# A third block's experts by routed rows: scatter to DRAM, 23 tiles of 128 rows, gather back

## The chip, the core and the metric

One core of one Trainium2 chip runs the whole program. The metric is the device time of one execution in microseconds, the median of several runs. PE is TensorE (matrix products and transpositions), PEld its weight loads, DVE is VectorE, ACT ScalarE, POOL GpSimd, SP SyncE, which here only issues DMAs.

## The reference

The input is one image of 32 x 32 tokens with 128 channels, so N = 1024 tokens, T = 8 tiles of P = 128. Three blocks of attention and mixing follow each other, then the fourth: a plain attention over 1024 tokens with its own experts. The change concerns the experts of the third block, `_L2_ffn_ref`:

```python
logits = xt @ Wr + br                                  # E = 8 experts
probs = softmax(logits); top_p, top_idx = top_k(probs, 2)
weights = top_p / top_p.sum(axis=-1, keepdims=True)
xn = layer_norm(xt)                                    # no gain
xe = xn[None] * ln_g[:, None, :] + ln_b[:, None, :]    # gain and bias per expert
h = gelu(einsum('end,edh->enh', xe, W1) + b1)          # 128 -> 512
y = einsum('enh,ehd->end', h, W2) + b2                 # 512 -> 128
out = sum over the token's two experts of weights * y[expert, token]
```

All experts are written as computed for all tokens, and only two of the eight results of a token are used. Everything is float32.

## The kernel before, in words

There is one instruction list per engine, written out by hand; the engines meet at semaphores (`wait_ge` on `at(name, k)`). Within an engine the order in the list is the order of execution. Operations of DVE or POOL that depend on each other go through `link`, which waits for each one's end.

The experts of the third block are computed densely. `tokens_to_channels` turns the tokens of the normalised block input (`bK`, for the router) and of the second normalisation (`cK`, for the experts), `router` makes the logits in one PSUM bank, and `router_logits`, `rank_experts` and the lines after them on DVE make `cw`, a weight for each token and expert that is zero for all but two experts.

For each expert the input is `nT` times the expert's gain plus its bias. Both this input (1024 columns) and the first matrix (128 x 512) are split into a high and a low part, so that a product is three passes of a fast number format with 512 columns (`PASSES`): ACT makes the high part of the input, POOL the whole input (`m2_xe`, line 649) and the high part of the matrix (line 484), DVE the low parts (`x_low`, `w_low`). `experts` on PE runs the first product of expert e and then the second product of expert e - 1 (`fc2`), in plain float32, 4 calls of 128 columns for each token tile. ACT evaluates the gelu (line 847) from PSUM into `hid(e)`. `accumulate` on DVE adds `cw` times the result to the residual `aK` (line 1905) for each expert and tile, and after the last expert makes the statistics of the next normalisation (`nc`). In the trace a call of PE in float32 is two records; `mm` is line 933, `turn4` line 943.

SP loads all second matrices (2 MB, line 410) and all first ones (2 MB, line 412) during the second block, and, expert by expert as a buffer comes free, those of the fourth block's experts (lines 417 and 419).

POOL's queue around the change: it splits the heads of the third block's attention, makes the high parts, the roots of the normalisations (`token_roots`, line 463), then small tables for the fourth block, and the roots of `nc`.

Two operations of the second block read a register from SBUF and use it as an address, as the change does: `split_stacks` on POOL (`value_load` of `topi`, then line 556) and `gather_keys` on DVE (line 1717).

After the experts PE turns the normalised tokens, makes queries, keys and values for the fourth attention, and goes on as before; the change leaves that part as it is. `warm` are products without use, which keep PE's clock up.

Of the kernel before, what the change touches and what calls it, by code (L numbers as in the profile page):

```python
# [5 lines left out]
P = 128  # L6
IMG = 32
T = IMG * IMG // P
N = T * P
# [34 lines left out]
U = 64  # L44
# [6 lines left out]
BIG = 3.0e38  # L51

# [18 lines left out]
for _name, _cols in (("n0_q_b", 4), ("n0_k_b", 4), ("n1_q_b", 4), ("n1_k_b", 4), ("L0_conv_proj_b", 1),  # L71
# [22 lines left out]
                  ("nn_tps", 2), ("nd_tps", 2)],  # L94
# [4 lines left out]
                   ("nb_T", 2), ("m2_xT", 2), ("nd_T", 2)],  # L99
# [29 lines left out]
for _kind, _count in (("lg_ps", 2), ("lg", 1), ("ex", 1)):  # L129
    KINDS["expert_" + _kind] = [(f"m2_{_kind}", _count), (f"m3_{_kind}", _count)]  # L130
# [23 lines left out]
def build(nc, A, out):  # L154
    with ExitStack() as ctx:
# [150 lines left out]
        lmask = sb("lmask", [P, T], U8)  # L306
        nanm = sb("nanm", [P, T, P], U8)
# [6 lines left out]
        xpart2 = kr[:, :, :].rearrange("p (b a) n -> p b a n", b=2)  # L314
        wpart2 = qr[:, :, :, :].rearrange("p b (a c) n -> p b a (c n)", a=2)
# [68 lines left out]
        def hid(e):  # L384
            return arena[:, 4096 * (e % 2):4096 * (e % 2) + 4096].rearrange("p (c n) -> p c n", c=FC)
# [12 lines left out]
        def _(sp):  # L398
# [9 lines left out]
            sp.dma_start(fb2[:, :], A["fb2"]).then_inc(S("fb2_in"), 16)  # L408
            sp.wait_ge(*at("conv_ps", 2))
            sp.dma_start(fw2[:, :, :, :], A["m2_w2"]).then_inc(S("fw_in"), 16)  # L410
            sp.wait_ge(*at("n1_qm", T))
            sp.dma_start(fw1[:, :, :], A["m2_w1"]).then_inc(S("fw_in"), 16)

            for e in range(E):
                sp.wait_ge(*at("m2_w_high", e + 1))
                sp.wait_ge(*at("m2_w_low", e + 1))
                sp.dma_start(fw1[:, e, :], A["m3_w1"][:, e]).then_inc(S("fv_in"), 16)
                sp.wait_ge(*at("m2_fc2", 2 * (e + 1)))
                sp.dma_start(fw2[:, e, :, :], A["m3_w2"][:, e]).then_inc(S("fv_in"), 16)
# [7 lines left out]
        def _(pool):  # L427
# [202 lines left out]
            def w_high(e):  # L630

                if e == 0:
                    pool.wait_ge(*at("fw_in", 32))
                if e >= 2:
                    pool.wait_ge(*at("m2_fc1", 8 * (e - 1)))
                copy(wpart2[:, e % 2, 0, :], fw1[:, e, :]).then_inc(S("m2_w_high"), 1)

            w_high(0)
            w_high(1)
# [3 lines left out]
            for e in range(E):  # L643
                dst = (bT, cT)[e % 2]
                if e == 0:
                    pool.wait_ge(*at("m2_xT", 2))
                if e >= 2:
                    pool.wait_ge(*at("m2_x_low", e - 1))
                pool.tensor_scalar(dst[:, :], nT[:, :], col("L2_ffn_ln_g", e), col("L2_ffn_ln_b", e),
                                   ALU.mult, ALU.add).then_inc(S("m2_xe"), 1)  # L650
                if 1 <= e < E - 1:
                    w_high(e + 1)

            def count(dst, pattern, mult):
                return pool.iota(dst, pattern, base=0, channel_multiplier=mult, allow_small_or_imprecise_dtypes=True)
# [9 lines left out]
            pool.wait_ge(*at("m2_fc1", 8 * E))  # L665
            pool.memset(k_high[U:U + 1, :].bitcast(F32), 1.0).then_inc(S("n3_ones"), 1)
            pool.wait_ge(*at("n3_ones", 1))
            token_roots("nc")
# [23 lines left out]
        def _(act):  # L692
# [130 lines left out]
            def router_exp(pre):  # L823
                act.wait_ge(*at(f"{pre}_lg", 1))
                act.activation(ex[:, :, :], lg[:, :, :], ACT.Exp).then_inc(S(f"{pre}_ex"), 1)

            def expert_layer(pre, func):

                def x_high(e):

# [1281 lines left out]
```

## Time and profile before

| | us |
|---|---|
| median of 3 runs | 537.44 |
| lowest, highest | 537.29, 545.58 |
| the profiled execution | 541.85 |
| its span, first to last instruction | 539.7 |
| PE busy in the span | 482.6 (89%) |
| mean granted clock of TensorE | 0.94 of 2.4 GHz |

The profile is of one execution on this core. Times in the rows are from the start of the span, in microseconds unless marked. "Busy" leaves out register, semaphore and DMA-issuing instructions. What stands in square brackets behind an instruction is the idle time of its engine before it and what ended it.

### The profile page before, as it was taken

The page shows a single profiled execution, that of the slowest core. Times are in us where ns is not written, and L with a number is a line of the kernel's source. Part 1 is how long each engine was busy: PE and PEld are TensorE (multiplying, and loading weights), DVE is VectorE, ACT ScalarE, POOL GpSimd, SP SyncE. Part 2 cuts the span into 40 slices and gives each one's busy share as a digit, 9 for nine tenths or more (in the row PEclk, how much of TensorE's full clock was granted, in tenths as well). Part 3 has the DMA queues.
Part 4 walks back from the last instruction along what each step waited for, and adds up shares of the span by engine and source line. Part 5 has one row for each costly group of instructions (what it writes and reads, how often), then busy time and mean ns, then how long its engine had stood idle before and what let it go on. Part 6 is the DMA issues. An engine that isn't in the chain of part 4 may idle for free.

```text
span 539.7 us, 9856 instructions
## 1 busy us (share of the span) xinstructions
PE 482.6 (89%) x3723; PEld 360.1 (67%) x3723; DVE 313.4 (58%) x830; ACT 243.4 (45%) x473; POOL 132.9 (25%) x187
## 2 busy tenths in 40 slices
PE   4988999795999999975886899999999999979994
PEld 3276676433677677763575789999998444567983
DVE  3858787478856668828366742233216531367367
ACT  0838877173355555640263495444440223310630
POOL 7622236004413323213331321112003300021000
PEclk9999999799799999997799699999999958979998
DMA  8000000000000000034000001111112000000001
GB/s 292 4 2 2 1 2 1 1 2 1 1 1 2 1 1 2 2 130 182 2 1 2 19 1 41 40 39 40 40 40 58 1 0 0 2 0 0 2 1 39
DMA packets 4680, 13.49 MB, mean 25 GB/s; under 512 B 466, under 2 KB 1562, under 8 KB 4250
## 3 DMA queue, kind: packets, MB, share of 16 engines
q1 hardware_dynamic: 4634, 12.86, 7.0%
q8 instruction: 30, 0.49, 0.4%
q14 instruction: 16, 0.13, 0.1%
HBM read 12.34 MB, written 0.52 MB: 24 GB/s over the span
## 4 chain that ended last, share of the span: by engine, by line
PE 75%; DVE 14%; ACT 4%; issue 3%; POOL 2%; DMA 1%; DVEq 1%; POOLq 0%; ACTq 0%
PE ps L933 68%; PE ps L1076 3%; DVE tabs L1568 2%; PE ps L943 2%; DVE st L1552 1%; PE ps L1056 1%; POOL rstd L463 1%; DVE arena L1690 1%; DMA xT<-in_xT_dram 1%; DVE oK L1666 1%; ACT arena L812 1%; DVE nmx L1830 1%; DVE arena L1827 1%; DVEq L1716 1%; PE ps L1047 1%
## 5 line engine op out<-in xcount | busy, mean ns | idle before, releaser
L933 PE MATMUL ps<-kr,qr 128*128 128x512 f32 (+3 forms) x328 | 92.8, 399 | 6.1 <-DVE kr L1717 2.4
L933 PEld LDWEIGHTS ps<-kr,qr 128*128 128x128 f32 x328 | 61.1, 193 | 22.8 <-issue 6.5
L847 ACT ACTIVATE arena<-ps,first 128x512 f32<-128x512 f32 x64 | 42.6, 689 | 38.5 <-PE ps L933 38.5
L933 PEld LDWEIGHTS ps<-fw,arena 128*128 128x128 f32 x512 | 58.3, 192 | 0.6
L933 PE MATMUL ps<-fw,arena 128*128 128x128 f32 x512 | 58.3, 275 | 0.0
L1786 DVE TENSOR_REDUCE nmx<-ps 128x1 f32<-128x512 f32 x64 | 43.8, 686 | 22.2 <-PE ps L933 21.7
L799 ACT ACTIVATE pT<-ps 128x512 f32<-128x512 f32 x64 | 38.3, 598 | 39.9 <-PE ps L933 39.3
L1905 DVE SCALAR_TENSOR_TENSOR aK<-ps,cw,aK 128x128 f32<-128x128 f32 x64 | 18.0, 344 | 63.4 <-PE ps L933 63.4
L463 POOL TENSOR_TENSOR rstd<-ve,nhalf 128x4 f32<-128x4 f32 x14 | 14.2, 1016 | 102.2 <-DVE ve L1561 102.1
L933 PE MATMUL ps<-kr 128*128 128x512 f32 x76 | 37.4, 582 | 1.0 <-ACT kr L910 1.0
L1690 DVE CUSTOM_DVE_ANT_0 arena<-ps,tabs 128x320 f32<-128x320 f32 (+1 forms) x64 | 28.8, 459 | 14.7 <-PE ps L933 14.7
L933 PE MATMUL ps<-pT,tabs 128*32 128x128 f32 (+2 forms) x576 | 35.6, 295 | 0.7 <-ACT pT L799 0.7
L762 ACT ACTIVATE arena<-arena,nmx 128x320 f32<-128x320 f32 (+1 forms) x64 | 32.2, 534 | 1.9 <-DVE nmx L1690 1.9
L1076 PE MATMUL ps<-ident,arena 128*64 128x128 f32 (+2 forms) x176 | 30.3, 277 | 1.1 <-ACT arena L762 0.5
L933 PE MATMUL ps<-first 128*128 128x256 f32 x98 | 30.2, 464 | 1.1 <-ACT arena L750 0.7
L715 ACT ACTIVATE pT<-ps,lowbias,islow 128x512 fp32r<-128x512 f32 x32 | 24.6, 778 | 12.8 <-PE ps L933 10.9
L556 POOL TENSOR_TENSOR tabs<-vaug,ones 128x151 f32<-128x151 f32 x32 | 14.3, 447 | 64.5 <-PE ps L933 36.7
L933 PEld LDWEIGHTS ps<-kr 128*128 128x128 f32 x76 | 16.3, 221 | 19.3 <-issue 16.3
L933 PEld LDWEIGHTS ps<-first 128*128 128x128 f32 x98 | 22.2, 237 | 4.8 <-ACT arena L750 0.9
L537 POOL TENSOR_TENSOR qr<-fw,mask 128x1024 fp32r<-128x1024 f32 x8 | 15.2, 1895 | 40.6 <-PE ps L933 35.8
L933 PEld LDWEIGHTS ps<-pT,tabs 128*32 128x32 f32 (+2 forms) x576 | 18.3, 111 | 6.6 <-issue 2.0
L933 PE MATMUL ps<-kv_high,convw_high 128*128 128x512 f32 x50 | 22.1, 442 | 0.0
(311 smaller groups left out, 937.2 us busy)
## 6 DMA issues: line engine op xcount, KB each, us to landing
fw<-in_m_w_dram SPq DMA_DIRECT2D x2, 2048.0 KB, 10.3
fw<-in_m_w_dram SPq DMA_DIRECT2D x16, 256.0 KB, 3.0
convw<-in_convw_dram SPq DMA_DIRECT2D x1, 1600.0 KB, 10.5
rows<-in_rows_dram SPq DMA_DIRECT2D x1, 584.0 KB, 6.1
xT<-in_xT_dram SPq DMA_DIRECT2D x1, 512.0 KB, 3.6
out_dram<-aK SPq DMA_DIRECT2D x2, 256.0 KB, 2.3
w<-in_w_dram SPq DMA_DIRECT2D x1, 448.0 KB, 6.9
late<-in_late_dram SPq DMA_DIRECT2D x1, 360.0 KB, 10.9
```

Of the source, the lines that this page charges most:

```text
L463: pool.tensor_tensor(dst, src, nhalf[:, 0:n], ALU.pow).then_inc(S(f"{name}_root"), 1)
L537: pool.tensor_tensor(dst.rearrange("p (g a) n -> p g a n", a=2), qst[:, :, P * t:P * t + P].unsqueeze(2).broadcast_to([P, 4, 2, P]), mask[ ...
L556: pool.tensor_tensor(vfil[:, t % 2, j:j + 1, :], vaug[:, bass.ds(r, 1), :], ones[:, 0:1].unsqueeze(2).broadcast_to([P, 1, VW]), ALU.mult). ...
L715: act.activation(pT[:, u % 4, :].bitcast(F32R), ps[:, u % 4, :], ACT.Identity, bias=lowbias[:, layer, a, k:k + 1], scale=islow[:, low:low ...
L762: act.activation(v, v, ACT.Exp, bias=nmx[:, t, h:h + 1], scale=-1.0).then_inc(S("n0_p"), 1)
L799: act.activation(pT[:, u % 8, :], ps[:, 4 + u % 2, :], ACT.Exp).then_inc(S("n1_p"), 1)
L847: act.activation(hid(e)[:, c // 2, HALF * (c % 2):HALF * (c % 2) + HALF], ps[:, c % 4, :], func, bias=col("L2_ffn_b1", FC * e + c // 2)).t ...
L933: return pe.matmul(dst, lhsT, rhs, start=start, stop=stop, skip_group_check=True)
L1076: ins = pe.transpose(ps[0:n, 4 + m % 2, P * j:P * j + P], arena_s(m // NH8)[:, m % NH8, P * j:P * j + n], ident[:, :])
L1690: dve.tensor_tensor_reduce(arena_s(t)[:, h, 0:w], ps[:, s % 4, 0:w], tab[:, h, :, :].rearrange("p l j -> p (l j)"), -1.0, FMAX, ALU.add, A ...
L1786: dve.tensor_reduce(nmx[:, s // NH8, s % NH8:s % NH8 + 1], ps[:, s % N1_S, :], AX.X, ALU.max, negate=True).then_inc(S("n1_nmx"), 1)
L1905: dve.scalar_tensor_tensor(acc[:, t, :], ps[:, 4 + 2 * (e % 2) + t // 4, P * (t % 4):P * (t % 4) + P], cw[:, t, e:e + 1], acc[:, t, :], AL ...
```

## The change

The experts work on rows instead of on all tokens. A row is a token with one of its two experts, 2048 rows in all. Each expert's rows are padded to whole tiles of 128, at most (2 x 1024 + 8 x 127) // 128 = 23 tiles; 23 are always run.

1. Two tensors in DRAM are added: `x_dram`, 9 x 1024 rows of 128 (1024 for each expert), and `y_dram`, 23 x 128 rows. SP fills `x_dram` with zeros early in the program (4.7 MB).
2. DVE works out the routing in two halves of 4 tiles: for each token and expert its place among the expert's rows (PE sums over tokens with triangular and full matrices of ones, `m2_positions`), from it `row_of` for the scatter and, with the number of tiles of each expert, `back_of` for the gather, `tile_expert` and `tile_row` for each tile, and its gain, bias and first bias (`tables`, `rows_back`).
3. POOL sends the normalised rows `cK` to `x_dram` with 16 indirect DMAs of 128 rows (`send_rows`), 8 after each half.
4. SP loads the first matrix of the first 4 tiles (256 KB each, expert by register, `weights_in`) into a ring of 4 buffers, waits for all rows, loads 23 tiles of rows (64 KB, first row by register, 5 in flight), and then, tile by tile, the first matrix of tile i + 4 and the store of the result i.
5. PE turns the tile, and runs four calls of 128 columns for the first product and four for the second, all in plain float32, one step apart: turn s, first product s - 1, second product s - 2. It reads the expert of a tile into a register and uses it to address the second matrix. DVE applies gain and bias on the way out of PSUM, ACT the gelu, DVE copies the result.
6. When all 23 results are in DRAM, POOL gathers them with 16 indirect DMAs, and DVE adds them with their weights to `aK`, tile by tile, with the statistics of `nc`.
7. The dense products, the high and low parts and `accumulate` are gone. The fourth block's first matrices are loaded whole in place of the third's, its second ones after the last second product.

```diff
+            sp.wait_ge(*at("w3_sums", 1))
+            sp.dma_start(x_dram.rearrange("(a p) c -> p a c", p=P), fills[:, 0:1, :].broadcast_to([P, XROWS // P, P])
+                         ).then_inc(S("rows_zero"), 16)
             sp.wait_ge(*at("conv_ps", 2))
             sp.dma_start(fw2[:, :, :, :], A["m2_w2"]).then_inc(S("fw_in"), 16)
             sp.wait_ge(*at("n1_qm", T))
-            sp.dma_start(fw1[:, :, :], A["m2_w1"]).then_inc(S("fw_in"), 16)
-            for e in range(E):
...
+            sp.dma_start(fw1[:, :, :], A["m3_w1"]).then_inc(S("fv_in"), 16)
+            def weights_in(i):
+                if i >= W1_BUFS:
+                    sp.wait_ge(*at("m2_fc1", i - W1_BUFS + 1))
+                e = sp.value_load(tile_expert[0:1, i:i + 1], min_val=0, max_val=E - 1)
+                sp.dma_start(w1_of(i), A["m2_w1"][:, bass.ds(e, 1), :].rearrange("p a h -> p (a h)")
+                             ).then_inc(S(f"w1_in_{i % W1_BUFS}"), 16)
+            sp.wait_ge(*at("tile_row", 1))
+            for i in range(W1_BUFS):
+                weights_in(i)
+            sp.wait_ge(*at("rows_out", 16 * TOPK * T))
+            for i in range(NT):
+                if i >= IN_FLIGHT:
+                    sp.wait_ge(*at(f"rows_in_{i % IN_FLIGHT}", 16 * (i // IN_FLIGHT)))
+                sp.dma_start(x_rows[:, i, :], x_dram[bass.ds(tile_row_of(i), P), :]).then_inc(S(f"rows_in_{i % IN_FLIGHT}"), 16)
+            for i in range(NT):
+                if i + W1_BUFS < NT:
+                    weights_in(i + W1_BUFS)
+                sp.wait_ge(*at("m2_y", i + 1))
+                sp.dma_start(y_dram[P * i:P * i + P, :], y_rows[:, i, :]).then_inc(S("y_stored"), 16)
+            sp.wait_ge(*at("m2_fc2", NT))
+            sp.dma_start(fw2[:, :, :, :], A["m3_w2"]).then_inc(S("fv_in"), 16)
@@ POOL
+            def send_rows(i):
+                pool.wait_ge(*at("row_of", i + 1))
+                pool.wait_ge(*at("nn_norm", 4 * i + 4))
+                for t in range(4 * i, 4 * i + 4):
+                    for r in range(TOPK):
+                        pool.indirect_dma_start(out=x_dram[:, :], out_offset=bass.IndirectOffsetOnAxis(
+                            ap=row_of[:, r, t:t + 1], axis=0), in_=cK[:, t, :], in_offset=None,
+                            bounds_check=XROWS - 1, oob_is_err=False).then_inc(S("rows_out"), 16)
...
+            pool.wait_ge(*at("y_stored", 16 * NT))
+            for t in range(T):
+                for r in range(TOPK):
+                    pool.indirect_dma_start(out=y_back[:, r, t, :], out_offset=None, in_=y_dram[:, :],
+                                            in_offset=bass.IndirectOffsetOnAxis(ap=back_of[:, r, t:t + 1], axis=0),
+                                            bounds_check=NT * P - 1, oob_is_err=False).then_inc(S(f"y_back_{t // 2}"), 16)
@@ PE
+            for s in range(NT + 2):
+                if s < NT:
+                    pe.wait_ge(*at(f"rows_in_{s % IN_FLIGHT}", 16 * (s // IN_FLIGHT + 1)))
+                    if s >= 2:
+                        pe.wait_ge(*at("m2_xt", s - 1))
+                    pe.transpose(ps[:, s % 2, 0:P], x_rows[:, s, :], ident[:, :]).then_inc(S("m2_xt_ps"), 1)
+                    e_of[s] = pe.value_load(tile_expert[0:1, s:s + 1], min_val=0, max_val=E - 1)
+                i = s - 1
+                if 0 <= i < NT:
+                    pe.wait_ge(*at("m2_xt", i + 1))
+                    pe.wait_ge(*at(f"w1_in_{i % W1_BUFS}", 16 * (i // W1_BUFS + 1)))
...
+                    for c in range(FC):
+                        ins = mm(ps[:, 2 + i % 2, P * c:P * c + P], w1_of(i)[:, P * c:P * c + P],
+                                 x_turned[:, i % 2, :])
+                    ins.then_inc(S("m2_fc1"), 1)
+                i = s - 2
+                if 0 <= i < NT:
...
+                    pe.wait_ge(*at("m2_h", FC * (i + 1)))
+                    for c in range(FC):
+                        ins = mm(ps[:, 4 + i % 2, 0:P], hid[:, i % 2, c, :], fw2[:, bass.ds(e_of[i], 1), c, :],
+                                 start=c == 0, stop=c == FC - 1)
+                    ins.then_inc(S("m2_fc2"), 1)
@@ DVE, in this order
+            router_logits("m2", 0, 4, 0, 4, 1)
+            rank_half(0)
+            half_stats("nn", bK, 1, "nb")
+            normalise_half("nn", bK, cK, 0)
+            rows_of_half(0)
+            router_logits("m2", 0, 2, 4, T, 2)
+            rank_half(1)
+            normalise_half("nn", bK, cK, 1)
+            rows_of_half(1)
+            tables()
+            rows_back()
...
+            for s in range(NT + 2):
+                if s < NT:
+                    dve.wait_ge(*at("m2_xt_ps", s + 1))
...
+                    dve.tensor_scalar(x_turned[:, s % 2, :], ps[:, s % 2, 0:P], tile_gain[:, s:s + 1], tile_bias[:, s:s + 1],
+                                      ALU.mult, ALU.add).then_inc(S("m2_xt"), 1)
+                i = s - 2
+                if 0 <= i < NT:
+                    dve.wait_ge(*at("m2_fc2", i + 1))
+                    dve.tensor_copy(y_rows[:, i, :], ps[:, 4 + i % 2, 0:P]).then_inc(S("m2_y"), 1)
```

## Rows read from the trace of the kernel before

**Rows 1.** The page: PE's busy time, and the chain that ended last by engine
```profile
PE 482.6 (89%) x3723; PEld 360.1 (67%) x3723; DVE 313.4 (58%) x830; ACT 243.4 (45%) x473; POOL 132.9 (25%) x187
PE 75%; DVE 14%; ACT 4%; issue 3%; POOL 2%; DMA 1%; DVEq 1%; POOLq 0%; ACTq 0%
```

**Rows 2.** Stages: stretch and length, busy PE, PEld, DVE, ACT, POOL, clock, DMA, GB/s
```profile
310.80:412.40 101.60, 101.60 (x718) 93.71 (x719) 32.26 (x90) 49.40 (x71) 14.76 (x19) 1.00 0.13 37
```

**Rows 3.** Groups of PE from 310 to 413, by form: count, busy us, mean ns, idle
```profile
L933 PE MATMUL ps<-fw,arena 128*128 128x128 f32 x512 | 58.3, 275 | 0.0
L933 PE MATMUL ps<-kr,qr 128*128 128x512 f32 x180 | 43.3, 395 | 0.9 <-ACT arena L847 0.9
```

**Rows 4.** Timeline at both ends of the stage: start us, us, engine line operation
```profile
293.01 0.29 DVE L1843 TENSOR_TENSOR aK<-ps,aK 128x128 f32<-128x128 f32 x1 [0.31 <-PE ps L933]
297.45 0.87 DVE L1552 BATCH_NORM_STATS2 st<-tabs 128x6 f32<-128x128 f32 x4
298.10 1.72 PE L933 MATMUL ps<-late,oT 128*128 128x8 f32 x8
298.71 1.11 DVE L1568 TENSOR_SCALAR tabs<-tabs,mv,rstd 128x128 f32<-128x128 f32 x4
...
412.33 1.13 DVE L1905 SCALAR_TENSOR_TENSOR aK<-ps,cw,aK 128x128 f32<-128x128 f32 x4 [1.06 <-PE ps L933]
```

**Rows 5.** Timeline of DVE: two router operations and two of the ranking
```profile
307.95 0.22 DVE L1863 TENSOR_REDUCE lm<-lg 128x8 f32<-128x64 f32 x1
308.20 0.22 DVE L1864 TENSOR_TENSOR lg<-lg,lm 128x64 f32<-128x64 f32 x1
308.46 0.69 DVE L1873 TENSOR_TENSOR tabs<-lg 128x512 f32<-128x512 f32 x1
309.19 0.69 DVE L1874 TENSOR_TENSOR tabs<-tabs,tril 128x512 f32<-128x512 f32 x1
```

**Rows 6.** SP's DMA issues in the timeline, and by size with us to landing
```profile
329.54 0.33 SPq L419 DMA_DIRECT2D fw<-in_m_w_dram  x1
329.96 0.38 SPq L417 DMA_DIRECT2D fw<-in_m_w_dram  x1
...
fw<-in_m_w_dram SPq DMA_DIRECT2D x2, 2048.0 KB, 10.3
fw<-in_m_w_dram SPq DMA_DIRECT2D x16, 256.0 KB, 3.0
out_dram<-aK SPq DMA_DIRECT2D x2, 256.0 KB, 2.3
```

**Rows 7.** Registers read from SBUF, on POOL and DVE; POOL's operation on 128x1024
```profile
209.06 0.44 POOL L556 TENSOR_TENSOR tabs<-vaug,ones 128x151 f32<-128x151 f32 x1 [0.73 <-POOL tabs L556]
210.23 0.53 POOL L556 TENSOR_TENSOR tabs<-vaug,ones 128x151 f32<-128x151 f32 x1 [0.72 <-POOL tabs L556]
L1717 DVEq FUSED_REGOPS  x2: 69/69/69, 125.7 to 126.5; - x2
L537 POOL TENSOR_TENSOR qr<-fw,mask 128x1024 fp32r<-128x1024 f32 x8 | 15.2, 1895 | 40.6 <-PE ps L933 35.8
```

**Rows 8.** Timeline: four transpositions on PE, four 128-column operations on ACT
```profile
273.67 0.60 PE L943 MATMUL ps<-ident,arena 128*128 128x128 f32 x4
275.21 1.28 ACT L812 ACTIVATE arena<-arena,nmx 128x128 f32<-128x128 f32 x4 [1.86 <-DVE nmx L1830]
```

**Rows 9.** Stages of 5 us: PE's busy time is the second number, its clock third last
```profile
275.00:280.00 5.00, 4.26 (x39) 4.10 (x38) 3.05 (x9) 3.84 (x12) 2.27 (x3) 1.00 0.01 2
295.00:300.00 5.00, 3.12 (x17) 2.79 (x18) 4.70 (x28) 1.20 (x2) 2.67 (x3) 0.78 0.00 0
300.00:305.00 5.00, 4.83 (x19) 4.23 (x20) 2.98 (x7) 3.25 (x4) 1.90 (x2) 0.50 0.18 52
```

**Rows 10.** Timeline: a DVE cast beside a POOL operation that reads SBUF
```profile
126.90 2.99 POOL L545 TENSOR_TENSOR tabs_parts<-tabs,kv_high 128x1296 fp32r<-128x1296 f32 x1
127.02 3.15 DVE L1717 CAST kr<-arena 128x512 fp32r x1
```

More of the change, by code:

```diff
@@ L129 @@
 for _kind, _count in (("lg_ps", 2), ("lg", 1), ("ex", 1)):
-    KINDS["expert_" + _kind] = [(f"m2_{_kind}", _count), (f"m3_{_kind}", _count)]
+    KINDS["expert_" + _kind] = [(f"m2_{_kind}", 2 if _kind == "lg" else _count), (f"m3_{_kind}", _count)]
+for _kind, _first, _second in (("fc1", NT, 2 * E), ("fc2", NT, E), ("h", FC * NT, FC * E), ("y", NT, E)):
+    KINDS["expert_" + _kind] = [("m2_" + _kind, _first), ("m3_" + _kind, _second)]
+KINDS["constants"] = [("rpb_zero", 1), ("gavg_ready", 1), ("shift_ready", 1), ("ident_ready", 2), ("rmask_ready", 1),
+                      ("islow_ready", 1)]
+KINDS["gathered"] = [("m3_gathered", T), ("slotrow_ps", 1)]
+KINDS["hot_made"] = [("m3_hot_ready", T), ("m3_xg_dve", 1)]
+KINDS["slots_made"] = [("m3_before", 2), ("m3_slot", 1)]
+KINDS["route_ps"] = [("m2_pos", 2), ("m2_count", 1), ("m2_cwt_ps", 2), ("m2_b2_ps", 2), ("m3_pos", 1)]
+KINDS["m2_sums"] = [("m2_cw", 1), ("m2_b2", 2), ("m2_acc", T)]
+KINDS["n3_prepared"] = [("places_ready", 4), ("w3_twice", 1), ("n3_ones", 1), ("n3_k_high", 2)]
+KINDS["expert_chosen"] = [("m2_chosen", 2), ("m3_hot", 1)]
+KINDS["m2_tables"] = [("row_of", 2), ("tile_expert", 1), ("tile_row", 1), ("tile_b1", 1), ("back_of", 1)]
 for _group in (("ln1", "nb", "nc", "nd"), ("ln2", "nn")):
@@ L306, in build @@
         lmask = sb("lmask", [P, T], U8)
+        row_of = sb("row_of", [P, TOPK, T], U32)
+        back_of = sb("back_of", [P, TOPK, T], U32)
+        tile_expert = sb("tile_expert", [P, NT], U32)
+        tile_row = sb("tile_row", [P, NT], U32)
         nanm = sb("nanm", [P, T, P], U8)
@@ L1330, in _ @@
             warm(2, 5)
             tokens_to_channels("nb_tps", (0, 1), bK, "nb_norm")
-            router("m2", 0, 4, oT, "nb_T", range(0, 4))
-            tokens_to_channels("nn_tps", (2, 3), cK, "nn_norm")
-            router("m2", 0, 4, oT, "nb_T", range(4, T))
-            warm(2, 5)
-            pe.wait_ge(*at("m2_xT", 2))
-            def m2_w(e, second):
-                pe.wait_ge(*at("fw_in", 32))
-            def m2_parts(e):
-                for name in ("m2_x_high", "m2_x_low", "m2_w_high", "m2_w_low"):
-                    pe.wait_ge(*at(name, e + 1))
@@ L1345, in _ @@
-            experts("m2", m2_parts, m2_w)
+            for i in range(2):
+                router("m2", 0, 4 - 2 * i, oT, "nb_T", range(4 * i, 4 * i + 4))
+            for i in range(2):
+                m2_positions(i)
+            for i in range(2):
+                ins = mm(ps[:, 6, 0:E], ones[:, :], half_sum[:, i, :], start=i == 0, stop=i == 1)
+            ins.then_inc(S("m2_count"), 1)
+            pe.wait_ge(*at("m2_cw", 1))
+            for i in range(2):
+                for j in range(4):
+                    ins = pe.transpose(ps[0:E, 4 + i, P * j:P * j + P], cw[:, 4 * i + j, :], ident[:, :])
+                ins.then_inc(S("m2_cwt_ps"), 1)
@@ new lines, in rows_back @@
+            def rows_back():
+                link(dve.scalar_tensor_tensor(row_step, start_of, float(P), first_row, ALU.mult, ALU.subtract))
+                link(dve.tensor_tensor(row_terms, rank_is, row_step.unsqueeze(1).unsqueeze(1).broadcast_to([P, TOPK, T, E]),
+                                       ALU.mult))
+                link(dve.tensor_reduce(weight, row_terms, AX.X, ALU.add))
+                dve.tensor_tensor(back_of[:, :, :], row_no, weight, ALU.add).then_inc(S("back_of"), 1)
+                dve.wait_ge(*at("back_of", 1))
```

357 lines of the change are left out of this document (188 added, 169 removed).

## The prediction

> **What bounds the kernel now.** I read the page's busy line and its chain first, then the stages, the groups of PE, and the timeline at both ends of the stage that is replaced. PE is busy 89% of the span and holds 75% of the chain that ended last [rows 1]: what PE does not do in this kernel is saved, as long as nothing else takes the time. The third block's experts are the stretch 310.8 to 412.4: PE is busy in all 101.6 us of it, at a granted clock of 1.00 (2.4 GHz), with DVE at a third and ACT at a half [rows 2]. Its work is 256 calls of the second product (512 records, 58.3 us, so 0.228 us a call) and 192 products of 512 columns, mostly in 43.3 us [rows 3]. The stage begins earlier on the other engines: the last residual of the attention is added at 293.01, the router's first half is out of PE at 298.10 + 1.72 = 299.8 at a low clock, and the last accumulation starts at 412.33 [rows 4]. I work the new course out on this clock and compare its end with 412.33.
>
> **What goes.** All of the dense products, the splits into high and low parts, and eight accumulations per tile. The time from the router's logits to the last accumulation, 412.33 - 299.8 = 112.5 us, is what the new course has to beat.
>
> **Row numbers on DVE.** A small operation on 64 elements takes 0.22 and starts 0.25 apart; one on 512 takes 0.69 and starts 0.73 apart [rows 5]. For 256 elements I estimate 0.45, between them. Each half of the router: three small (0.75), five of 256 (2.25), three small (0.75), together 3.75; then four operations for the rows, 1.0. The first half also has the statistics of the second normalisation, 1.27, and each half four normalised tiles, 1.11 [rows 4]. So the first row numbers are ready at 299.8 + 3.75 + 1.27 + 1.11 + 1.0 = 307.0, the second at 307.0 + 3.75 + 1.11 + 1.0 = 312.9. The tables follow: tile_expert and tile_row after 11 operations of 0.27, at 315.9; biases, rows_back and weights about 6.6 more, 322.5; for the transposed weights and their product with the second bias, PE, ACT and DVE in turn, I allow 5 us. DVE enters the tile loop at about 327.4. That is under the scatter, and costs nothing unless the scatter ends before 325.
>
> **Scatter.** POOL issues 16 indirect DMAs, one after another on its queue. The trace has none. The nearest rows are SP's plain DMA issues, 0.33 and 0.38, with starts 0.42 apart [rows 6], and POOL's gather of values, which reads a register out of SBUF and runs one operation: starts 1.17 apart, of which 0.73 is idle before it [rows 7]. An indirect DMA must read 128 numbers and write descriptors for them, so 0.42 is the low end; the high end, 2.0, is by POOL's slowest frequent operation, the one on 128x1024 at 1.90 [rows 7]. I take 1.2, near the row that also reads an index. Eight from 307.0 end at 316.6, past the second half's 312.9, so all 16 end at 307.0 + 19.2 = 326.2; with a landing of 2.3, the store's row [rows 6], the rows are in DRAM at 328.5.
>
> The Trainium skill, "DMA: Bandwidth & Descriptors", section "Latency and other measured facts", gives a first byte of about 1 us on this path, with the Q7's emission as its reason. No row here shows it. If 1.0 were the spacing, the sum below would be 6.4 us lower.
>
> **Loads of the rows.** The part that I think least visible: SP issues all 23 row loads before it issues weight 4. Each reads a register from SBUF and then issues a DMA that uses it. I put the register at 0.7: it is the 0.73 that POOL stands before the operation that follows one, and DVE's queue, which does the same, shows its register operations 0.8 apart, 125.7 and 126.5 [rows 7]. With an issue of 0.38 [rows 6] and a short wait that makes 1.15 a load, bounds 0.75 (the read partly hidden) and 1.4. 23 x 1.15 = 26.5, so 355.0; weight 4 is issued at 356.1 and lands 3.0 later, as 256 KB did [rows 6], at 359.1. Tiles 0 to 3 run below this and then PE stands for some 15 us. Five loads in flight are enough: five spacings are 5.75, a landing 2.3.
>
> **The tile loop.** Per tile PE has one transposition and eight calls of 128 columns: 8 x 0.228 + 0.11 = 1.94, the 0.11 from four transpositions that take 0.60 with 0.27 of it for the first [rows 8]. ACT has four gelus of 128 columns, 1.28 for four such operations [rows 8]; DVE two evacuations of 0.29 [rows 4]; SP one register, two issues and waits, 1.6; the 256 KB of a weight at the rate of the 2 MB load (10.3 us [rows 6]) 1.3. All lie below PE. PE must also read a register and form addresses: 0.65 or more, hidden as far as the sequencer runs ahead of eight queued products. No row shows PE do this. I take 0.46 of it as seen, so 2.4 a tile, bounds 1.94 and 3.0. From fc1(4) to fc2(22) are 19.5 tiles: 46.8. PE comes out of a stand, and the 5 us after one like it were granted 0.50 [rows 9], which loses some 2 us. End of fc2(22): 359.1 + 46.8 + 2 = 407.9. Evacuation, store issue and landing, 0.3 + 0.4 + 2.3: all y are in DRAM at 410.9.
>
> **Gather.** 16 indirect DMAs again, and all of them wait for the last store: 19.2 + 2.3 = 21.5, so 432.4. The accumulation of the last two tiles and their statistics, about 2.4, answer to the 2.5 that now follows 412.33 [rows 4]. So the stage ends 432.4 - 412.3 = 20.1 later. PE has stood meanwhile: the next attention's first 5 us at 0.50 cost 2.5 more [rows 9]. Sum: +22.6.
>
> The Trainium skill, "SBUF — State Buffer", section "SBUF: two separate sides", has a passage on DVE blocking DMAs from the GpSimd queue: a DVE operation that holds the shared ports keeps the descriptors from being written. The trace shows the lock from the other side, a cast taking 3.15 beside a POOL operation of 2.99 [rows 10]. By that rule the DVE operations beside the scatter and the gather, 16 of about 0.34 in the gather, would add at most 5 us; I leave it out of the sum.
>
> **Nothing for the rest.** The zeroing of the scatter's buffer (4.7 MB) is issued when the first loads are out and PE has 200 us of other work before rows are sent; at the rate above it takes 24 us of the DMA engines, idle there. The last block's 2 MB are loaded whole, 10.3 us, long before 500. Five iotas on POOL, 1 us, lie below DVE's attention work.
>
> **From the profile to the metric.** The profiled execution took 541.85: a span of 539.7 and 2.15 around it. The median is 537.44, 4.4 less. 541.85 + 22.6 = 564.4, less 4.4: 560.0 us. A measurement of this kernel tells about 2% from no change: 526.7 and 548.2.
>
> **Rivals.**
> - *Cheap indirect DMAs (not slower).* Place: POOL's queue, from the first row number to the last gather. If one costs what SP's issue does, 0.42, the scatter ends at 312.9 + 3.4 = 316.3, row loads end at 345.1, y is stored at 401.0, the last gather landed at 410.2: 2 us less than now, plus 2.5 of clock, 538 us. Each 0.1 us is 3.2 us of the total; below 0.83 the result is within 2%. With SP's loads at 0.75 (-9) and PE at 1.94 (-9) as well it is 519. For it: no POOL DMA is in the trace, so nothing excludes it. Against: 128 numbers per DMA, and the 0.73 for one [rows 7].
> - *Dear indirect DMAs*, 2.0: 32 x 0.8 = +25.6, 585 us.
> - *The tile loop loses the clock.* A stretch with PE busy 3.12 of 5 us was followed by one at 0.50, 4.26 of 5 kept 1.00 [rows 9]. At 2.4 a tile PE is busy 81%; at 3.0 it is 65%, and half clock makes the work 3.9. At a mean of 3.3 the loop is 17.6 longer: 578 us.
> - *Row loads overlap*: if SP's registers run ahead, 0.75 a load, 9.2 less: 551 us.
> - The loop's counts are constants, so routing cannot make it shorter, and that it does not do what it says I do not reckon with.
>
> **Chances.** Forecast 0.44, cheap 0.20 (0.09 of it faster by over 2%), dear 0.14, clock 0.11, overlapping loads 0.11 (half of it within 2%). The forecast's own low tail gives 0.04 to no change. Faster 0.09, within 2% 0.20, slower 0.71. The range reaches down past the cheap rival to 532 and up past the dear one to 588. The forecast's own is 549 to 574.
>
> **What would show it.** Right: POOL's indirect DMAs 1.2 apart, 16 before and 16 after the loop; SP's row loads 1.15 apart with PE idle some 15 us after tile 3; PE's tiles 2.4 apart at clock 1.00 with DVE, ACT and the DMA engines waiting; the last accumulation some 20 us later than 412.33 [rows 4]. Wrong: indirect DMAs under 0.8 apart; PE without a gap between tiles 3 and 4; a loop that waits for weights, so that the transfers and not PE set its pitch; tiles over 3 apart.

## The result, and the profile after

The changed kernel takes 555.46 us (median of 4 executions, 553.21 to 557.58) beside 538.33 for the kernel before: a ratio of 1.033, interval 1.029 to 1.037. The forecast was 560.0, range 532 to 588, slower. Run once more, later, it took 555.12 (553.91 to 566.9), ratio 1.031 [1.026, 1.036]. Some executions of most versions here are over 1.5% longer than the version's shortest, at a lower granted clock of TensorE; the ratios leave these out and the medians do not, so where they are many, as in a version below, the two say different things.

The page of the kernel after, PE's busy line and the chain that ended last by engine, answers to [rows 1]:

```profile
PE 438.6 (79%) x3420; PEld 323.3 (58%) x3420; DVE 314.4 (57%) x858; ACT 217.1 (39%) x491; POOL 151.4 (27%) x208
PE 64%; DVE 14%; issue 7%; POOL 4%; SPq 4%; ACT 3%; DMA 2%; DVEq 1%; POOLq 0%
```

PE does 44 us less work (482.6 before) and the kernel is 16 us longer: 60 us went into stretches in which PE stands. The chain says who holds it there: "issue", time in which an engine waits for nothing that the profile shows, rose from 3% to 7%, POOL from 2% to 4%, and SPq, SP's queue, is new with 4%, some 22 us.

I measure the stage from the last residual add of the attention before it to the last variance (`ve`) behind it: 293.01 to 414.68 before, 121.7 us; 299.08 to 436.20 after, 137.1 us. The stages of the kernel after inside it (columns as in [rows 2]):

```profile
299.10:314.30 15.20, 8.98 (x36) 7.49 (x35) 11.62 (x55) 1.45 (x3) 3.06 (x4) 0.50 0.00 0
314.30:339.90 25.60, 8.73 (x38) 7.42 (x39) 14.51 (x45) 1.17 (x2) 20.13 (x22) 0.50 0.28 85
339.90:351.80 11.90, 9.64 (x62) 8.47 (x62) 2.55 (x8) 5.60 (x17) 0.00 (x0) 0.81 0.21 58
351.80:367.60 15.80, 0.05 (x1) 0.08 (x1) 0.51 (x2) 0.15 (x1) 0.00 (x0) 0.59 0.27 74
367.60:408.50 40.90, 40.37 (x330) 39.17 (x331) 10.98 (x36) 21.73 (x76) 0.00 (x0) 0.95 0.53 149
408.50:436.20 27.70, 3.03 (x15) 2.32 (x13) 9.55 (x34) 0.00 (x0) 17.23 (x17) 0.64 0.35 116
```

Read the second number, PE's busy time, against the length. Routing, scatter (POOL busy 20.1), tiles 0 to 3, a stretch of 15.8 in which the computing engines do nearly nothing (0.7 busy in all), 19 tiles at PE's own pace (40.4 of 40.9), gather (POOL 17.2). Of 137 us PE works 71; before it worked 117 of 122. It stands in three stretches above all: 16.9 us beside the scatter, 15.8 behind tile 3, 24.7 in the gather. POOL's timeline has the scatter (first fence) and the gather (second):

```profile
314.26 1.47 POOL L736 DMA_INDIRECT expert_rows_dram<-tabs,row_of  x1 [1.79 <-issue]
...
323.72 0.97 POOL L736 DMA_INDIRECT expert_rows_dram<-tabs,row_of  x1 [0.30 <-issue]
325.00 1.95 POOL L736 DMA_INDIRECT expert_rows_dram<-tabs,row_of  x1 [0.30 <-issue]
327.26 1.04 POOL L736 DMA_INDIRECT expert_rows_dram<-tabs,row_of  x1 [0.30 <-issue]
...
334.98 0.97 POOL L736 DMA_INDIRECT expert_rows_dram<-tabs,row_of  x1 [0.30 <-issue]
```

```profile
411.33 1.11 POOL L758 DMA_INDIRECT arena<-expert_out_dram,back_of  x1 [72.18 <-DMA expert_out_dram<-arena]
412.74 1.01 POOL L758 DMA_INDIRECT arena<-expert_out_dram,back_of  x1 [0.31 <-issue]
...
431.09 0.99 POOL L758 DMA_INDIRECT arena<-expert_out_dram,back_of  x1 [0.30 <-issue]
```

Most scatters start 1.28 us apart (0.97 busy, 0.30 between), gathers 1.30; the first scatter takes 1.47 and the ninth 1.95. SP's timeline and then PE's show the row loads and the stand that they make; where the timeline merges instructions, the second number spans all of them:

```profile
338.00 25.78 SPq L502 DMA_DIRECT2D arena<-expert_rows_dram  x23
364.56 0.33 SPq L492 DMA_DIRECT2D xT<-in_m_w_dram  x1
```

```profile
351.50 0.27 PE L1394 MATMUL ps<-ident,arena 128*128 128x128 f32 x1
367.55 2.05 PE L1007 MATMUL ps<-arena,xT 128*128 128x128 f32 x8 [15.77 <-DMA xT<-in_m_w_dram]
...
378.30 1.06 PE L1007 MATMUL ps<-fw,arena 128*128 x8
379.19 0.27 PE L1394 MATMUL ps<-ident,arena 128*128 128x128 f32 x1
380.24 1.06 PE L1007 MATMUL ps<-fw,arena 128*128 x8
381.13 0.27 PE L1394 MATMUL ps<-ident,arena 128*128 128x128 f32 x1
```

23 row loads, 1.157 us apart; the weight of tile 4 behind the last; PE idle 15.77 us for it. From the second one on, a transposition every 1.89 to 2.10 us.

Outside the stage the two profiles differ too: the stage begins 6.1 us later (299.08 against 293.01), and from the last variance to the end it is 119.4 us, not 125.0. 15.4 + 6.1 - 5.6 = 15.9, the whole difference of the spans (555.6 - 539.7). The runs below had to tell which of these three belongs to the change.

### The profile page after: what moved, and what is told of

Same layout as the page of the kernel before. It is cut to its first block, busy times and chain, and to the rows that moved or that the text cites. A ratio compares the mean times of both kernels' runs of the same rounds, so it can differ in the third digit from the quotient of the medians.

```text
span 555.6 us, 9834 instructions
## 1 busy us (share of the span) xinstructions
PE 438.6 (79%) x3420; PEld 323.3 (58%) x3420; DVE 314.4 (57%) x858; ACT 217.1 (39%) x491; POOL 151.4 (27%) x208
## 3 DMA queue, kind: packets, MB, share of 16 engines
q1 hardware_dynamic: 21642, 24.53, 13.9%
q0 software_dynamic: 1024, 2.10, 1.3%
## 4 chain that ended last, share of the span: by engine, by line
PE 64%; DVE 14%; issue 7%; POOL 4%; SPq 4%; ACT 3%; DMA 2%; DVEq 1%; POOLq 0%
PE ps L1007 57%; PE ps L1150 3%; POOL arena L758 2%; SPq L485 2%; PE ps L1017 2%; POOL expert_rows_dram L736 2%; SPq L502 2%; DVE tabs L1637 1%; DVE st L1621 1%; PE ps L1130 1%; DVE arena L1759 1%; ACT arena L905 1%; DMA xT<-in_xT_dram 1%; DVE nmx L1899 1%; DVE arena L1896 1%
## 5 line engine op out<-in xcount | busy, mean ns | idle before, releaser
L892 ACT ACTIVATE pT<-ps 128x512 f32<-128x512 f32 x64 | 38.3, 598 | 40.4 <-PE ps L1007 39.8
L1007 PE MATMUL ps<-kr,qr 128*128 128x320 f32 (+3 forms) x136 | 46.4, 404 | 4.4 <-DVE kr L1786 2.4
L931 ACT ACTIVATE arena<-ps,convw 128x128 f32<-128x128 f32 x92 | 26.2, 370 | 35.9 <-PE ps L1007 35.9
L758 POOL DMA_INDIRECT arena<-expert_out_dram,back_of x16 | 16.2, 1012 | 76.7 <-DMA expert_out_dram<-arena 72.2
L1017 PE MATMUL ps<-ident,tabs 128*128 128x128 f32 x40 | 8.6, 354 | 35.1 <-DVE tabs L1637 35.1
L2043 DVE COPY arena<-ps 128x128 f32<-128x128 f32 x23 | 6.7, 292 | 51.4 <-PE ps L1007 51.4
L1007 PEld LDWEIGHTS ps<-kr,qr 128*128 128x128 f32 x136 | 25.4, 197 | 13.2 <-issue 5.7
L1007 PE MATMUL ps<-kr 128*128 128x512 f32 x76 | 31.3, 498 | 1.0 <-ACT kr L984 1.0
L1007 PE MATMUL ps<-arena,xT 128*128 128x128 f32 x96 | 15.5, 313 | 16.1 <-DMA xT<-in_m_w_dram 15.8
L1017 PEld LDWEIGHTS ps<-ident,tabs 128*128 128x128 f32 x40 | 6.1, 182 | 38.0 <-issue 26.6
L627 POOL TENSOR_TENSOR qr<-fw,mask 128x1024 fp32r<-128x1024 f32 x8 | 15.1, 1893 | 45.4 <-PE ps L1007 39.9
L1007 PE MATMUL ps<-fw,arena 128*128 x184 | 25.4, 282 | 1.8 <-ACT arena L931 1.3
## 6 DMA issues: line engine op xcount, KB each, us to landing
expert_rows_dram<-fills SPq DMA_DIRECT2D x1, 4608.0 KB, 18.3
convw<-in_convw_dram SPq DMA_DIRECT2D x1, 1600.0 KB, 11.2
```

Source lines behind the costliest of these rows:

```text
L627: pool.tensor_tensor(dst.rearrange("p (g a) n -> p g a n", a=2), qst[:, :, P * t:P * t + P].unsqueeze(2).broadcast_to([P, 4, 2, P]), mask[ ...
L758: pool.indirect_dma_start(out=y_back[:, r, t, :], out_offset=None, in_=y_dram[:, :], in_offset=bass.IndirectOffsetOnAxis(ap=back_of[:, r, ...
L892: act.activation(pT[:, u % 8, :], ps[:, 4 + u % 2, :], ACT.Exp).then_inc(S("n1_p"), 1)
L931: act.activation(hid[:, i % 2, c, :], ps[:, 2 + i % 2, P * c:P * c + P], ACT.Gelu, bias=tile_b1[:, i, c:c + 1]).then_inc(S("m2_h"), 1)
L1007: return pe.matmul(dst, lhsT, rhs, start=start, stop=stop, skip_group_check=True)
L1017: ins = pe.transpose(ps[0:rows, bank, cols * j:cols * j + cols], src, ident[0:cols, 0:cols])
```

## The experiments

The first four versions ran beside executions of the kernel before with a median of 539.42.

**The zero fill moved.** SP's fill of `x_dram` is issued some 240 us in, not 22.

```diff
-            sp.dma_start(x_dram.rearrange(...), fills...).then_inc(S("rows_zero"), 16)
...
             sp.dma_start(fw1[:, :, :], A["m3_w1"]).then_inc(S("fv_in"), 16)
+            sp.dma_start(x_dram.rearrange(...), fills...).then_inc(S("rows_zero"), 16)
```

> The changed kernel with one edit: the 4.6 MB that zero the scatter's buffer are issued behind the two 2 MB loads, at about 243 us, instead of at 22 us. My theory: this transfer, in flight from 22 to 40 us, is why the first attention starts at 45.3 instead of 40.6 (a gap of 0.87 us on PE that nothing releases, then the 14 products without use at half clock, 6.3 us instead of 3.3). Then the first maximum is back at 40.6 and the total falls by 4 to 6 us, to about 550. Rival: the late start is a matter of chance in that execution, and the total stays at 555.

560.05 us (552.37 to 562.71), ratio 1.032 [1.022, 1.042]: no gain, and the theory's number did not come. Its profile did begin the stage at 292.36, 6.7 earlier than the changed kernel's, but its tail was 129.8, 10.4 longer. With four executions that far apart the run settled nothing; the last experiment takes it up again.

**Rows, weights and stores in turn.** SP loads five tiles of rows, and then for each tile weight, rows, store.

```diff
-            for i in range(NT):
-                (load rows i)
+            for i in range(IN_FLIGHT):
+                rows_in(i)
             for i in range(NT):
                 if i + W1_BUFS < NT:
                     weights_in(i + W1_BUFS)
+                if i + IN_FLIGHT < NT:
+                    rows_in(i + IN_FLIGHT)
                 sp.wait_ge(*at("m2_y", i + 1))
```

> The changed kernel, but SP issues only 5 row loads ahead and then, tile by tile, weight i + 4, rows i + 5 and the store of result i. My theory: PE's stand of 15.8 us after tile 3 comes from the 23 row loads issued ahead of weight 4. Then it goes, but SP becomes the bound with 1.17 + 1.1 + 0.43 = 2.7 us a tile against PE's 1.95, the last second product ends some 8 us earlier, and the total is about 547. Rival 1: SP's registers run ahead and PE's 1.95 stays the pace: 15 us less, 540. Rival 2: PE stands for something other than the order on SP: no change, 555.

554.87 us (545.64 to 562.66). The whole is too spread to tell, but the stage is not: 131.2 us against 137.1, and from the first transposition to the last second product 62.5 against 68.6: some 6 us earlier, where I expected 8. SP's timeline shows what replaced the stand:

```profile
353.92 0.33 SPq L492 DMA_DIRECT2D xT<-in_m_w_dram  x1
355.03 0.33 SPq L502 DMA_DIRECT2D arena<-expert_rows_dram  x1
355.41 0.52 SPq L511 DMA_DIRECT2D expert_out_dram<-arena  x1
356.70 0.33 SPq L492 DMA_DIRECT2D oT<-in_m_w_dram  x1
```

2.78 us from weight to weight, over the 1.95 that PE needs: two register reads and three issues are more than a tile's work, so SP paces the loop.

**Rows on POOL's queue.** The same loads, issued by POOL, which has some 3 us to do between scatter and gather.

```diff
@@ SP
-            for i in range(NT):
-                sp.dma_start(x_rows[:, i, :], x_dram[bass.ds(tile_row_of(i), P), :])...
@@ POOL, behind send_rows(1)
+            for i in range(NT):
+                r = pool.value_load(tile_row[0:1, i:i + 1], ...)
+                pool.dma_start(x_rows[:, i, :], x_dram[bass.ds(r, P), :])...
```

> The changed kernel, but the 23 row loads are issued by POOL, which has nothing to do then, and SP keeps weights and stores. If PE's stand is due to SP's queue alone, PE runs from the first tile to the last at its 1.95 us, POOL's pace of about 0.7 + 1.3 = 2.0 us a tile being as fast: 17 us less, about 538. Rival: a DMA that POOL makes with a register costs 2.5 us or more, and the loop is bound by it: at most 6 us less, 549.

541.34 us (10 executions, 537.04 to 552.95), ratio 1.002 [0.998, 1.006]: the loss is gone, with 538 expected. Its stage is 122.4 us, 14.7 less than the changed kernel's, and the loop 53.0 for 68.6. The timeline of POOL shows that the loads are no faster there (1.16 apart); only nobody waits behind them:

```profile
344.38 0.54 POOL L741 DMA_DIRECT2D arena<-expert_rows_dram  x1 [0.62 <-issue]
345.54 0.54 POOL L741 DMA_DIRECT2D arena<-expert_rows_dram  x1 [0.62 <-issue]
```

**A pause in the kernel before.** Is the 5.6 us in the tail a gift of the change, because PE rests in the gather before the next attention? The kernel before got a pause of 22 memsets on POOL at that place.

```diff
+            pool.wait_ge(*at("m2_acc", T * E))
+            for _ in range(22):
+                link(pool.memset(bT[:, :], 0.0))
             token_roots("nc")
```

> The kernel of before with a pause: POOL waits for the last accumulation of the third block's experts and then writes 22 times 1024 columns of an unused buffer, some 22 us, before the next roots. PE stands meanwhile, as it does during the gather. My theory: what PE did before decides the clock in the next attention, and after a rest that attention no longer falls to half clock (430 to 447 us before): from the last variance to the end it takes 119 to 120 us, as in the changed kernel, instead of 125. Rival: the rest only adds a cold start, and the same stretch takes 125 to 128 us.

570.57 us; the pause took 22.13, and the tail is 149.1, some 127 without it. From 460 to 470 us the granted clock was 0.50 with PE busy throughout: the rest did not keep the half clock away. This theory fell.

**Both kernels once more**, unedited.

> The changed kernel once more, nothing edited. Theory (the early part up to the first attention, 45.3 us in its first profile against 40.6 of before, and the tail, 119.4 against 125.0, are set by where the half-clock stretches fall in one execution and are no part of the change): in this profile at least one of the two differs from the first profile by over 2 us, while the stage from the last residual add to the last variance stays within 2 us of 137.1 apart from the clock at its start. Rival (the change itself moves them): again 45 and 119. The ratio to the kernel before: 1.033, 1.027 to 1.040.

> The kernel before once more, nothing edited. By the same theory the last residual add comes anywhere from 291 to 300 us and the tail is 119 to 130 us; by the rival they are 293 and 125 again. The stage from the last residual add to the last variance, whose matrix calls keep TensorE at work, stays at 121.7, within 2 us, if the clock in it is the same.

Here are the tails, from last variance to end: the kernel before in its first and second profile, then the kernel after in its two (first number the length, then PE's busy time; clock third last):

```profile
414.70:539.70 125.00, 109.87 (x471) 75.08 (x469) 64.97 (x143) 33.66 (x74) 14.85 (x12) 0.89 0.02 5
```

```profile
419.71:538.20 118.49, 103.77 (x471) 73.13 (x470) 64.86 (x143) 33.54 (x74) 14.84 (x12) 0.95 0.02 5
```

```profile
436.20:555.60 119.40, 104.54 (x468) 74.11 (x468) 64.96 (x143) 33.54 (x74) 14.82 (x12) 0.93 0.02 5
```

```profile
435.11:564.90 129.79, 114.93 (x468) 78.18 (x468) 64.86 (x143) 33.65 (x74) 14.87 (x12) 0.84 0.02 5
```

The same work in all four, DVE busy 64.9 in each, and what the tail has beside PE's busy time is 14.7 to 15.1 in each. PE's busy time is 104 to 115, the longer the lower the granted clock: the difference is the clock, and it changes between two executions of one kernel. The stages do not: 121.65 (before 121.7) and 137.29 (before 137.1). So +15.4 is the change's and -5.6 is not. The start of the stage: 298.06 for the kernel before now, 297.82 for the kernel after, so most of the +6.1 is not either.

**Half of the gather.** The second expert's rows are not fetched and its part is not added.

```diff
-                for r in range(TOPK):
+                for r in range(1):
                     pool.indirect_dma_start(out=y_back...
```

> Changed kernel with 8 of the 16 indirect gathers left out: the second expert's rows are not fetched and its weighted contribution is not added (8 accumulations of DVE fewer too). Theory (POOL's queue paces the end, 1.30 us for each gather): from the first gather to the last variance 24.87 us in the changed kernel (411.33 to 436.20) becomes 24.87 - 8 x 1.30 = 14.5. Rival (the latency of the transfers sets it and the pitch only fills it): under 3 us shorter. The remaining gathers' pitch stays 1.30.

From the first gather to the last variance 13.7 us (410.51 to 424.21) for 24.87: 11.2 less for eight gathers, 1.4 each, by the pitch of 1.30 and two DVE operations fewer behind the last. One execution, 545.22 us. POOL's queue paces the end.

**PE without its register.** The second matrix of tile i is matrix i modulo 8, so the routing's choice of it is left out.

```diff
-                    e_of[s] = pe.value_load(tile_expert[0:1, s:s + 1], ...)
...
-                                 fw2[:, bass.ds(e_of[i], 1), c, :]
+                                 fw2[:, i % E, c, :]
```

> Changed kernel in which TensorE reads no register and takes its second matrix by a constant (tile number modulo 8): the routing's choice of the second matrix is left out. Theory (the read is hidden behind queued matrix calls): the steady tile pitch stays 1.95 us, within 0.05, and the tiles' stretch as in the changed kernel. Rival (my prediction's term, 0.45 us a tile for read and addressing): a pitch near 1.5, or 23 x 0.45 = 10 us less, and at the least the pitch goes down to the 1.94 of bare work.

The ten tiles between DVE's copies at 371.34 and 391.17 of the changed kernel are 1.98 us apart; here, from 372.27 to 391.23, 1.90. The read costs no more than some 0.09 us of a tile where I had 0.46. How much less is not settled: two profiles of one later version that has the read show 1.96 and 1.91. One execution, 561.45 us.

**Results scattered in the loop.** The gathers can only start when the last result is stored. Here each routed row takes the number of its place (rank, token) along as a 129th float, and POOL scatters the result of a tile as soon as it is there; padding rows carry a number out of bounds and are skipped. Behind the loop 8 plain loads fetch all. SP loads the rows of even tiles, ACT those of odd ones.

```diff
@@ POOL, in the loop
+                pool.indirect_dma_start(out=y_dram[:, :], out_offset=bass.IndirectOffsetOnAxis(
+                    ap=x_rows[:, i, P:XW].bitcast(U32), axis=0), in_=y_rows[:, i % Y_BUFS, :], ...)
-            for t in range(T):
-                for r in range(TOPK):
-                    pool.indirect_dma_start(out=y_back[:, r, t, :], ..., in_=y_dram[:, :], ...)
@@ SP, behind the loop
+            for t in range(0, T, 2):
+                for r in range(TOPK):
+                    sp.dma_start(y_back[:, r, t:t + 2, :], back[:, r, t:t + 2, :])...
```

> Each routed row carries its destination number as a 129th float, so the result of a tile is sent to its place (rank, token) by an indirect scatter of POOL right after the tile; the 16 gathers at the end give way to 8 plain loads by SP. Row loads are issued by SP (even tiles) and ScalarE (odd tiles). Theory (POOL's queue is what counts, and in the loop it is idle): against the version with row loads on POOL (541.3 us) the end of the stage loses 16 x 1.30 = 20.8 us of gathers and gains a last scatter (about 1.3 + 2.3) and 8 plain issues (some 0.1 to 0.6 each), so about -11 to -15; the scatters in the loop at 1.3 stay under the tile pitch of 1.95 to 2.3. Forecast 528 us, 522 to 535: faster than the kernel before by 1 to 3%. Rival (the scatters of 23 tiles, 2944 rows of 512 bytes, pace the loop or the ring of four result tiles holds VectorE up): the loop goes to 2.6 us a tile or more, +7 to +10, and the whole is within 1% of the kernel before.

539.2 us (12 executions, 526.33 to 541.28) beside 540.03: ratio 0.982 [0.976, 0.988]. In the profile the stage is 107.4 us: 14 less than before, 30 less than in the changed kernel, and 15 less than with the rows on POOL, the far end of what I expected. The scatters keep up with PE:

```profile
362.95 0.97 POOL L781 DMA_INDIRECT expert_out_dram<-arena  x1 [1.05 <-DMA arena<-expert_rows_dram]
364.84 0.96 POOL L781 DMA_INDIRECT expert_out_dram<-arena  x1 [0.93 <-DMA arena<-expert_rows_dram]
366.85 0.96 POOL L781 DMA_INDIRECT expert_out_dram<-arena  x1 [1.05 <-DVE arena L2070]
```

But the median is where it was, not at the 528 of the forecast, and whether this version is faster stays unclear. The stage began at 301.2 and the tail was 130.8.

> The version with results scattered in the loop, unedited, once more, since its medians (539.2 against 540.0) and the ratio of the undisturbed executions (0.982) said different things. Theory (the stage is 14 us shorter in every execution, 107.4 against 121.7, and only the half-clock stretch after it, 10 to 11 us, comes and goes): the stage is 107 to 108 again, the tail 119 to 131, and the ratio 0.976 to 0.988. Rival (TensorE gets its half-clock stretch in the tail whenever the stage is shorter, so most executions give 11 of the 14 us back): tail 130 again and a ratio of 0.99 to 1.0.

538.97 us (529.97 to 541.99) beside 539.4, ratio 0.993 [0.988, 0.999]; stage 106.6, start 300.79, tail 129.7. The rival's numbers for tail and ratio came, so I looked for what else is the same in both profiles: the first attention starts at 47.9 and 47.5, in the kernel before at 40.6 and 42.9. PE's timeline there, first the kernel before, then the changed kernel, then this version:

```profile
34.19 0.94 PE L933 MATMUL ps<-w,arena 128*128 128x128 f32 x6 [0.68 <-ACT b_turned L747]
34.96 0.39 PE L933 MATMUL ps<-w,tabs 128*128 128x128 f32 x2
```

```profile
34.81 0.71 PE L1007 MATMUL ps<-w,arena 128*128 128x128 f32 x4 [0.68 <-ACT b_turned L840]
...
36.40 0.49 PE L1007 MATMUL ps<-w,arena 128*128 128x128 f32 x2 [0.87 <-issue]
```

```profile
34.26 0.71 PE L1042 MATMUL ps<-w,arena 128*128 128x128 f32 x4 [0.73 <-ACT b_turned L863]
...
38.35 0.79 PE L1042 MATMUL ps<-w,arena 128*128 128x128 f32 x2 [3.38 <-issue]
```

A group of six equal products runs through in the five profiles without the early fill. With it, PE stands after the fourth, waiting for nothing that the profile shows: 0.53 to 0.87 us in the six profiles with rows of 128, 2.99 and 3.38 in the two with rows of 129, whose fill took 32.9 and 32.2 us to land and not 18.3. It does so while the fill keeps the DMA engines busy (share 0.94 from 30 to 40 us in the changed kernel, 0.01 before).

The trace has more on this than the timeline: it lists each packet of the DMA engines with its kind. Without the early fill a packet of 16 KB of the kind "instruction" starts at 29.8 to 30.6 us. With it the same packet starts at 33.3 to 34.3 us, in the wide form at 35.5 and 36.4, and in all eight profiles PE goes on 1.25 to 1.50 us after it has ended. That fits instructions of PE which come late behind the fill. No run moves this packet alone, so it is not shown.

What the stand does to the start of the stage differs by form. The stage begins at 292.4 to 298.1 us in the five profiles without the early fill, at 293.3 to 299.1 in the six with the narrow one, and at 300.8 and 301.2 with the wide one. So the last version has the fill late again.

```diff
-            sp.dma_start(x_dram.rearrange(...), fills_wide...).then_inc(S("rows_zero"), 16)
...
             sp.dma_start(fw1[:, :, :], A["m3_w1"]).then_inc(S("fv_in"), 16)
+            sp.dma_start(x_dram.rearrange(...), fills_wide...).then_inc(S("rows_zero"), 16)
```

> The version with results scattered in the loop, with the zero fill of its 9216 rows issued some 240 us in, behind the load of the fourth block's first matrices, in place of 22 us in. Theory (while the fill runs, TensorE stands 3.0 to 3.4 us in the middle of a group of products at 35 us, waiting for nothing that the profile shows, and comes out of it at half clock, so the first attention starts at 47.5 to 47.9 in place of 40.6 to 42.9): that stand is gone, the first attention starts at 41 to 43, the last residual add comes at 292 to 297 in place of 301, and the whole is 4 to 6 us shorter: 534 us, ratio 0.978 to 0.990 against all executions of before. Rival (the stand moves with the fill): a stand of 1 to 4 us on TensorE between 240 and 285 us and no gain of over 2 us.

523.14 us (6 executions, 521.31 to 532.09) beside 539.82: ratio 0.970 [0.967, 0.973], faster than the kernel before by 3%, and more than I expected (534). The stand is gone and does not come back at 240 us: PE's "issue" of 0.43 there stands in the version with the early fill, and in the kernel before, too (first line: fill late, second: fill early).

```profile
34.18 0.94 PE L1042 MATMUL ps<-w,arena 128*128 128x128 f32 x6 [0.68 <-ACT b_turned L863]
...
243.63 3.54 PE L1042 MATMUL ps<-first 128*128 128x256 f32 x8 [0.43 <-issue]
```

```profile
250.83 3.65 PE L1042 MATMUL ps<-first 128*128 128x256 f32 x8 [0.43 <-issue]
```

The first attention starts at 40.6, the stage at 294.04, is 107.8 long, and the tail is 120.5. Of the 14.8 us that its span is under that of the execution of the second run (522.3 against 537.1), 6.75 are gained before the stage and 9.2 behind it, and 1.2 lost in it. What I can show is that the stand goes with the early fill; that the half-clock stretch in the tail goes with it too is what one profile and the narrow spread of six executions suggest, not more. The five shortest of the 24 executions with the early fill took 526.3 to 531.8, five of the six here 521.3 to 525.5: some 5 us, about what is gained before the stage. In the first experiment, the same edit of the changed kernel left the tail at 129.8.

## Why the prediction was right, and where not

The verdict, the time (555.5 for 560.0) and the mechanism came as forecast: queues of POOL and SP that PE waits behind. That the time is so near is in part luck, because terms of both signs cancel. Against the steps, all from the start of the stage:

- *Row numbers*: first ones 14.0 us behind the last residual add by the working; `row_of` was there at 13.9 (312.98). The first scatter came 1.3 us later still, at the end of 1.79 of "issue" on POOL, which I did not have.
- *Scatter*: 1.2 each, measured 1.28, but the first took 1.47 and the ninth 1.95. From the first to the first row load 23.7 for 21.5.
- *Row loads*: 1.15 each, measured 1.157; PE's stand "some 15 us", measured 15.77. This was the term that I thought least visible, and with the loads elsewhere 14.7 of the 15.4 are gone. It does not carry the loss alone: it is one of three stretches in which PE stands, and taking the gathers out of the end as well gave another 15 (122.4 to 107.4).
- *Tile loop*: the term that was mis-sized. "I take 0.46 of it as seen, so 2.4 a tile" measured 1.98, of which the register read is 0.09 at most. The 0.65 for the read, from which the 0.46 was taken, came from no row. From weight 4 to the last second product 40.9 us for 48.8: 7.9 too many, the largest miss. The half clock behind the stand, 2 us, was there (2.05 for eight products of the first tile, 1.06 later).
- *Gather*: 19.2 for the queue, measured 20.8; up to the last variance 24.9 for 24.0.
- *Sum of the stage*: +20.1 forecast, +15.4 measured. Too low were the first scatter (1.2), scatter to row loads (2.2) and gather (1.0); too high the tile loop (7.9), row loads and the landing of weight 4 (29.6 for 30.6) and the last store (2.8 for 3.0). 4.4 under and 9.1 over leave 4.7 too many.
- *Cold next attention*, +2.5: not to be seen. The tail moves by 10 us between two executions of one kernel, so this term lies under what one profile can say.
- *"Nothing for the rest"*: wrong for the zero fill. I asked whether anybody needs the DMA engines while it runs, and named PE's 200 us of other work as cover. PE itself stood 0.5 to 0.9 us in it, and in the wider form 3.0 to 3.4. The 24 us that I gave the fill were 18.3, and 32.9 in the wider form. On the changed kernel the effect is lost in the spread; with the wide fill moved, the median fell by 16 us, of which the profile shows 6.75 before the stage and the rest in a tail that changes by itself.
- *Profile to metric*: I took 4.4 off to get from the profiled execution to the median; of after, the profiled execution is 557.58, 2.1 over its median. The forecast for the profiled execution, 564.4, was 6.8 too high; the 4.4, of which 2.1 came, brought the miss down to 4.5. Inside the 6.8, a start 6.1 later and a tail 5.6 shorter, neither forecast, cancel.

The rivals: cheap indirect DMAs (0.42) and dear ones (2.0) are excluded by 1.28 and 1.30. The loop kept its clock, 0.95 over its 40.9 us. Row loads did not overlap. That a DVE operation which holds the shared ports keeps an indirect DMA waiting (the Trainium skill, "SBUF — State Buffer", section "SBUF: two separate sides") fits one scatter: the one of 1.95 at 325.00 lies beside two DVE operations on 736 elements, of which the first took 1.47 and the second 0.92. It is also the first of its half, in every run, so no run tells the two causes apart. Of the others only the very first scatter (1.47) and the first gather (1.11) are over 0.1 longer than the rest, so it was right to leave the term out of the sum. The first-byte figure of about 1 us, which the Trainium skill gives in "DMA: Bandwidth & Descriptors", section "Latency and other measured facts", is near the 0.97 that POOL is busy with one; the pitch has 0.30 more.

What stays open: why the half-clock stretch in the last attention comes in some executions and not in others, and whether it is the late instruction packet through which the fill holds PE.

## What to carry to other kernels

Before work is cut on the busiest engine, add up what the new course puts on the queues of the idle ones, in order: here 44 us less of matrix work lost to 16 scatters and 16 gathers on POOL and 23 loads in front of one weight on SP. The loads and the gathers were in order of convenience: the loads cost nothing on a queue that nobody waits behind, and the gather becomes a scatter under the loop once each row carries its own address. A big background transfer is not free because no one needs its data: put it where the engines do not stop in it, and look at the "issue" gaps of the main engine while it runs.

## What the runs showed that I had not expected

- An indirect DMA of 128 rows of 512 bytes mostly holds POOL 0.97 to 1.01 us, and the next starts 1.28 to 1.30 after it, scatter or gather.
- A register read from SBUF and a DMA that uses it: 1.157 us on SP, 1.16 on POOL. On PE the read costs at most some 0.09 of a 1.98 us tile.
- A DMA fill to DRAM of 516-byte rows took 32.9 and 32.2 us to land where one of 512-byte rows took 18.3, with 1% more bytes; issued late, behind two loads of 2 MB, 41.5 for 26.6.
- The tail takes 118.5 to 120.5 us in some profiles and 125.0 to 130.8 in others. It changes in one kernel from one execution to the next (118.5 and 125.0; 119.4 and 129.8), and there by the granted clock alone.
